# A binarised 3x3 convolution after group norm: a pair's two half convolutions side by side on TensorE, one more input slot, thresholds on GpSimd

## What is computed

```python
def _gn(v, G=32, eps=1e-05):          # G == C: one group is one channel of one image
    ...
    return ((g - m) / jnp.sqrt(s + eps)).reshape(v.shape)

def _L0_conv_ref(X, W, beta, v, bias, stride):
    B = jnp.sign(W[None] - mean + us[:, None, None, None, None] * std)   # 5 sign filters
    alpha = jnp.linalg.solve(Bf.T @ Bf, Bf.T @ wf)
    W_eff = jnp.einsum('m,mhwio->hwio', alpha, B)
    ...
    for n in range(3):
        An = jnp.sign(jnp.clip(X + v[n], 0.0, 1.0) - 0.5)
        out = out + beta[n] * (conv(An) + sum_alpha * bias[n])
    return out

x = x + _L0_conv_ref(_gn(x), ...)
```

## Time and profile before

| | before |
|---|---|
| median of 3 runs | 194.65 us (194.5 to 195.14) |
| the profiled execution | 194.47 us, of it the span of the profile 192.7 us |
| busy: TensorE, VectorE, ScalarE, GpSimd | 90%, 85%, 80%, 29% of the span |
| DMA over the span | 39.6 MB, mean 206 GB/s |

### The profile page before, as it was taken

How to read it: one execution, slowest core, us unless ns; L and a number is a source line. 1 busy time by engine, 2 the same in 40 slices (tenths; PEclk the granted TensorE clock), 3 DMA queues, 4 the chain that set the end, 5 groups by cost and what they waited for, 6 DMA issues and landing times.

```text
span 192.7 us, 4809 instructions
## 1 busy us (share of the span) xinstructions
PE 174.0 (90%) x1828; PEld 133.8 (69%) x1828; DVE 163.3 (85%) x409; ACT 154.2 (80%) x221; POOL 55.1 (29%) x72
## 2 busy tenths in 40 slices
PE   1898988749999999999899989999989999999992
PEld 1687765634868787868677777878777857677671
DVE  5579995999999999999988999899999899975242
ACT  2719968998898989999998989998988898872131
POOL 6264010006060606060605051323232242434000
PEclk9999999997999999999999999999999999999999
DMA  5999990063598989799988798989883837677725
GB/s 160 246 236 241 250 229 18 2 173 99 146 226 248 237 282 243 231 227 301 254 263 235 227 252 252 231 253 250 259 242 112 236 100 201 177 211 210 224 76 167
DMA packets 20476, 39.60 MB, mean 206 GB/s; under 512 B 9078, under 2 KB 9302, under 8 KB 20454
## 3 DMA queue, kind: packets, MB, share of 16 engines
q1 hardware_dynamic: 20144, 39.27, 74.8%
q10 hardware_dynamic: 310, 0.04, 0.1%
HBM read 13.15 MB, written 12.85 MB: 135 GB/s over the span
## 4 chain that ended last, share of the span: by engine, by line
PE 59%; DVE 18%; DMA 11%; ACT 7%; issue 2%; SPq 2%; DVEq 0%
PE conv_ps L843 33%; PE y_ps L876 10%; DMA s_odd<-s_even 10%; PE x_ps L795 6%; DVE raw_stats L629 5%; ACT signs L372 3%; DVE y_nat L620 3%; PE conv_ps L851 3%; DVE s_even L682 3%; PE conv_ps L846 2%; ACT x_ch L367 1%; ACT w_parts L413 1%; SPq L225 1%; ACT filt L410 1%; PE conv_ps L931 1%
## 5 line engine op out<-in xcount | busy, mean ns | idle before, releaser
L843 PE MATMUL conv_ps<-s_even,w_mm 128*64 128x448 f16 (+1 forms) x576 | 104.3, 335 | 3.5 <-DMA s_odd<-s_even 2.5
L846 PE MATMUL conv_ps<-s_odd,w_mm 128*64 128x448 f16 (+2 forms) x576 | 104.4, 323 | 0.0
L372 ACT ACTIVATE signs<-x_ch,neg_thr 128x784 f16<-128x784 f32 x96 | 85.3, 939 | 0.5
L843 PEld LDWEIGHTS conv_ps<-s_even,w_mm 128*64 128x64 f16 x576 | 60.6, 110 | 31.8 <-issue 10.3
L846 PEld LDWEIGHTS conv_ps<-s_odd,w_mm 128*64 128x64 f16 x576 | 60.8, 111 | 0.1
L335 POOL TENSOR_SCALAR lo_part<-signs,ratio_lo 128x1568 f16<-128x1568 f16 x14 | 22.0, 1575 | 103.1 <-DVE half_hi L675 103.1
L385 ACT ACTIVATE y_ch<-conv_ps,y_scale 128x896 f32<-128x896 f32 (+1 forms) x31 | 28.3, 911 | 17.6 <-PE conv_ps L851 10.3
L620 DVE SCALAR_TENSOR_TENSOR y_nat<-y_ps,y_const,x_nat 112x1024 f32<-112x1024 f32 (+1 forms) x30 | 34.4, 1148 | 8.3 <-PE y_ps L876 8.0
L629 DVE BATCH_NORM_STATS2 raw_stats<-x_ch 128x6 f32<-128x448 f32 (+1 forms) x64 | 31.6, 554 | 0.8 <-ACT x_ch L367 0.8
L876 PE MATMUL y_ps<-ident,y_ch 128*112 128x128 f32 x210 | 29.0, 278 | 0.0
L795 PE MATMUL x_ps<-ident,x_nat 112*128 112x112 f32 x192 | 25.5, 277 | 2.1 <-DMA x_nat<-in_x 1.4
(11 more groups left out here) (126 smaller groups left out, 126.7 us busy)
## 6 DMA issues: line engine op xcount, KB each, us to landing
x_nat<-in_x SPq DMA_DIRECT2D x16, 448.0 KB, 5.9
out<-y_nat SPq DMA_DIRECT2D x16, 448.0 KB, 5.9
s_odd<-s_even SPq DMA_DIRECT2D x32, 203.0 KB, 3.4
s_odd<-s_even SPq DMA_DIRECT2D x32, 188.5 KB, 3.8
x_nat<-in_x SPq DMA_DIRECT2D x16, 336.0 KB, 4.8
out<-y_nat SPq DMA_DIRECT2D x15, 322.0 KB, 2.9
s_odd<-s_even SPq DMA_DIRECT2D x16, 29.0 KB, 3.3
x_nat<-in_x SPq DMA_DIRECT2D x16, 14.0 KB, 5.9
```

What stands on the lines that cost most here:

```text
L372: act.activation(signs[q % 2][:, n, :, a, :], x_ch[q % CH_SLOTS][:, :, a, :], ACT.Sign, bias=neg_thr[q % 2][:, n, a:a + 1]).then_inc(signe ...
L843: last = nc.tensor.matmul(low[:, 0:n * ROWS], wt, s_even[b][:, part, r0:r0 + 2 * n, t:t + H], start=first, stop=end)
L846: last = nc.tensor.matmul(high[:, 0:m * ROWS], wt, s_odd[b][:, part, r0:r0 + 2 * m, t:t + H], start=first, stop=end and not at_edge)
```

## The change

The loop is written anew on all engines. A step on TensorE is now: half A of pair p, half B of pair p, statistics of pair p + 3, half B of pair p - 1 out, half B of pair p + 4 in (through `conv_ps[0]`, which half A has left), half A of pair p + 5 in, half A of pair p out. So all float16 matmuls of a pair stand together and all float32 work stands together, and half B leaves one period later; `y_ch` of half B has two buffers for that. The zero columns of `s_even` and `s_odd` are gone (rows of 56): the outer taps read and write 55 of 56 positions, and which tap starts and ends a bank is chosen so that it covers all of them. The two additions on VectorE write whole rows. The thresholds are computed on GpSimd (`thresholds`: one addition, one product, one sum and two `tensor_scalar`, L333 to L341) from the root and its inverse; VectorE keeps only the inverse. GpSimd's low part of a pair waits for `signed` and for `weigh_second` in place of `sum_half`. `x_nat` has 8 slots in place of 7, and the loop ahead of the steps loads all of them.

```diff
-X_SLOTS, CH_SLOTS, S_SLOTS = 7, 4, 3
+X_SLOTS, CH_SLOTS, S_SLOTS = 8, 4, 3
...
             for q in range(1, X_SLOTS):
                 load_x(q, 0)
                 load_x(q, 1)
...
+            def thresholds(q):
+                pool.wait_ge(moments_ready, 2 * (q + 1))
+                ts(var_eps[:], moments[q % 2][:, :, 1], GN_EPS, 1.0, ALU.add, ALU.mult).then_inc(pool_dev, 1)
+                pool.wait_ge(inverse_root, q + 1)
+                pool.wait_ge(pool_dev, 3 * q + 1)
+                tt(ratio_root[:], var_eps[:], inv_root[:], ALU.mult).then_inc(pool_dev, 1)
+                pool.wait_ge(pool_dev, 3 * q + 2)
+                tt(twice_dev[:], ratio_root[:], root[:], ALU.add).then_inc(pool_dev, 1)
+                pool.wait_ge(pool_dev, 3 * q + 3)
+                for a in range(2):
+                    ts(neg_thr[q % 2][:, :, a], order[:, 1, :], twice_dev[:, a:a + 1], moments[q % 2][:, a, 0:1],
+                       ALU.mult, ALU.add).then_inc(thr_ready, 1)
...
             for q in range(2, PAIRS):
-                weigh_low(q)
+                weigh_low_first(q)
+                weigh_low_second(q)
+                if q + 1 < PAIRS:
+                    thresholds(q + 1)
...
+            TAP_ORDER = [(1, 0, 2), (1, 0, 2), (0, 2, 1)]
+            TAP_OUT = [slice(1, H), slice(0, H), slice(0, H - 1)]
+            TAP_IN = [slice(0, H - 1), slice(0, H), slice(1, H)]
...
             def bring_out(p, f, ps=y_ps):
                 k = 2 * p + f
                 pe.wait_ge(y_scaled, k + 1)
                 if k:
                     pe.wait_ge(y_added, k)
-                if f == 0 and real(p - 1) and real(p + 3):
+                if f == 0 and real(p + 3):
                     pe.wait_ge(moments_ready, 2 * (p + 4))
...
             def step(p):
-                r, t = p + 3, p + 4
+                convolve(p, 0)
+                if p == 0:
+                    gather_lanes(2)
+                    pe.wait_ge(moments_ready, 6)
+                    bring_in(4, 0, x_ps, 7)
...
+                convolve(p, 1)
+                if p and real(p + 3):
+                    gather_lanes(p + 3)
+                if real(p - 1):
+                    bring_out(p - 1, 1)
+                if real(p + 4):
+                    pe.wait_ge(y_scaled, 2 * p + 1)
+                    bring_in(p + 4, 1, conv_ps[0], 0)
+                if real(p + 5):
+                    bring_in(p + 5, 0, x_ps, 2 * (p + 4) + 1)
+                if p == 0:
+                    gather_lanes(3)
+                bring_out(p, 0)
```

The steps of VectorE, ScalarE and SP follow the same period:

```diff
             def step(p):                     # VectorE
+                if real(p - 1):
+                    add_x(p - 1, 0)
+                if real(p + 1):
+                    sum_high(p + 1)
+                    sum_low(p + 1)
+                if real(p + 3):
+                    lane_moments(p + 3, 0)
+                    lane_moments(p + 3, 1)
+                    spread_lanes(p + 3)
+                if real(p + 2):
+                    weigh_first(p + 2)
+                    weigh_second(p + 2)
+                if real(p - 1):
+                    add_x(p - 1, 1)
+                if real(p + 3):
+                    pair_moments(p + 3)
+                if real(p + 2):
+                    sum_half(p + 2)
+                if real(p + 3):
+                    invert_root(p + 3)
...
             def step(p):                     # ScalarE
+                if real(p + 1):
+                    sign(p + 1, 0)
...
+                if real(p + 4):
+                    copy_in(p + 4, 0)
+                if real(p + 2):
+                    begin_signs(p + 2)
...
+                scale_out(p, 0)
+                if real(p + 2):
+                    sign(p + 2, 2)
...
+                    scale_out(p, 1)
+                if real(p + 4):
+                    copy_in(p + 4, 1, conv_ps[0])
+                if real(p + 3):
+                    take_root(p + 3)
```

More of the change, by code:

```diff
@@ L465, in _ @@
             copy_in(3, 0)
-            for p in range(-1, PAIRS):
+            take_root(2)
+            for p in range(PAIRS):
                 step(p)
@@ L778, in _ @@
             output_const()
-            for p in range(-1, PAIRS):
+            weigh_first(1)
+            pair_moments(2)
+            weigh_second(1)
+            sum_half(1)
+            invert_root(2)
+            weigh_low(1, 1)
+            weigh_low(1, 2)
+            for p in range(PAIRS):
                 step(p)
+            add_x(LAST, 0, x_ps)
+            add_last(0)
+            add_last(1)
         @block.tensor
@@ L957, in _ @@
             warm_up()
-            for p in range(-1, PAIRS):
+            bring_in(3, 1, y_ps, 6)
+            for p in range(PAIRS):
                 step(p)
```

231 lines of the change are left out of this document (80 added, 151 removed).

## The result

The changed kernel takes **218.4 us** (median of 4 runs, 217.94 to 222.01) against 194.89 for the kernel before beside it: a ratio of 1.120, 95% interval 1.114 to 1.126. It is slower, as forecast, but by 23.5 us where the forecast said 2.5. The time lies far outside the range of 194.2 to 200.8.

A forecast was written before the change was run, and what follows sets the result against it. Bound: a two-pair loop of TensorE, VectorE and the copy to s_odd. Copies -3.3, eighth slot +3.3, clock +0.7, rest of first periods -0.2, last periods +2.1, end -0.1: +2.5, median 197.1 us, range 194.2 to 200.8.

The forecast's parts named there:

- The thresholds: GpSimd in the loop: five small instructions run beside the rest on an otherwise unused engine, at a cost of nothing.
- (d): Rival, VectorE in the loop: half sum loses 0.5 us per period to GpSimd's product, total 200.4; chance 0.10.
- TensorE's own period: TensorE in the loop: fewer type switches (-0.18) and no zero columns (-0.07) bring the period from 9.67 to 9.42 us.
- the wait ahead of A's output: TensorE in the loop: moments of pair p + 3 need 2.14 us against 2.18 of work, a tie, 0.05 added.
- The copies: Copies to s_odd behind queued loads: 9.65 us for eight periods, 9.47 for two; -3.3 us, ends -4.8 and -0.3.
- The eighth slot: Start of pair 0: one more load queued ahead of its second copy delays half A; +3.3 us, ends 0 and 3.5.
- The clock: First periods: the half-clock dip in A of pair 1 recurs, a new one may come; +0.7 us, between 0 and 1.3.
- pair 0 to pair 2: First two periods: clock +0.7 us, and -0.2 for the rest, with four small VectorE instructions less.
- Rival (c): TensorE in the loop: float32 work in one piece brings a 1.3 us clock dip every third period, 203 us; chance 0.10.
- The last periods: End of the loop: B's output, its addition and A's output follow each other on one buffer, uncovered; +2.1 us.
- what is behind the last half A: End of the kernel, after the last half A: the order stays; -0.1 us.

The follow-up runs named there:

- thr_back: Changed kernel with the thresholds made on VectorE and ScalarE again, as before the change; 197.91 us, ratio 1.011 to the kernel before.
- thr_ahead: Changed kernel with GpSimd's thresholds ahead of both low products and VectorE's statistics ahead of its two sums; 202.49 us.
- tb_pads: thr_back with the zero columns kept (rows of 58, every tap on all 56 positions); 200.44 us, ratio 1.017.
- slots7: Changed kernel with seven input slots in place of eight; 217.18 us, ratio 1.113 to the kernel before.
- tb_tail7: thr_back with seven input slots and, in the last periods, half B's output in x_ps; 194.92 us, ratio 0.997.
- twice3: Changed kernel with GpSimd's small sum for the thresholds made three times in a row in every pair; 227.25 us, ratio 1.165.
- b_thr_pool: Kernel before the change with only the thresholds moved to GpSimd, behind both low products; 239.22 us, ratio 1.228.
- thr_stats: Changed kernel with thresholds between GpSimd's two low products and statistics ahead of VectorE's two sums; 204.67 us, ratio 1.035.
- stats_first: Changed kernel with only VectorE's order altered, statistics ahead of the two sums; 206.71 us, ratio 1.058.

## Why the prediction was wrong, step by step

**The thresholds (taken at nothing, measured 20.5 us).** This is the step that failed: "The thresholds' own five small instructions run beside these on GpSimd, which nothing else uses then." It asked whether GpSimd was free, not what stands ahead of them in its queue. Ahead stands the second product, which waits for the second weight, which waits for signs made from the thresholds of one pair earlier. That is a loop over one pair. The trace of before held all its pieces but the small ones, and it was never added up. The thresholds moved back give 20.5 us back (thr_back), and in the undisturbed periods another place in the queue does so too (thr_ahead). The rival on GpSimd's side (d) had the right pair of engines and the wrong victim: the half sum does lose 0.5 us (1.45 for 0.92), but the loop is set by the small instructions that VectorE holds. The earlier trace rows showed the hold on VectorE, 1.1 us; I never turned it round. The Trainium skill ("SBUF — State Buffer", "Who interferes with whom") says that whoever issues first has the shared pair for the whole instruction and that a `tensor_scalar` in a two-port mode takes it as well. The held weights of 1.63 and 1.73 us agree; the earlier trace rows alone didn't show that case. That the first to issue has the pair isn't seen in the threshold instruction, which by the recorded starts was 0.40 us ahead of the sum that held it.

**TensorE's own period (forecast 9.42 and a wait of 0.05, measured 9.60).** The work came out as forecast, and the wait ahead of A's output is what was mis-sized. In thr_ahead (TensorE's weight loads, then VectorE):

```profile
108.84 0.81 PEld L803 LDWEIGHTS x_ps<-ident,x_nat 112*128 112x128 f32 x8
109.89 0.84 PEld L891 LDWEIGHTS y_ps<-ident,y_ch 128*112 128x112 f32 x8 [0.24 <-issue]
```

```profile
109.50 0.28 DVE L670 BATCH_NORM_AGGREGATE moments<-y_ps 128x2 f32<-128x12 f32 x2
```

The moments are done at 109.78 and the output starts 0.11 us later, with 0.24 us of nothing to load before it; it is the same, within 0.01 us, in every period with both inputs in thr_ahead and thr_back. From the start of B's output to that of A's it takes 2.24 us (107.68 to 109.92), where the forecast had 2.14. TensorE's own work in it is 0.68 + 0.58 + 0.77 = 2.03, where the forecast had 2.18. The near tie is a wait of 0.2 us, and without it the period would be 9.4. Of what was won, the columns are 0.09 (tb_pads). That this wait makes the 9.60 is read from the traces; no run takes it away.

**The copies (forecast 9.65 for eight periods).** In thr_back, where this step can be seen, ten periods took 97.80 against the 96.1 of the forecast: the term is -1.7, within its ends. But its reason was wrong. TensorE waited for a copy once in ten periods, for 0.6 us, while VectorE was busy for 94.72 of 97.80. In seven of the ten, TensorE's weight loads wait for VectorE's statistics:

```profile
PEld y_ps L816 <- DVE spread_stats L647: 2.0, 7, 0.4
```

The upper end of -0.3 was not worked out: eight periods of 9.87 us, the forecast's own worst, and two of 9.47 give -1.6. That the measured size lies beside this is luck.

**The eighth slot (forecast +3.3, ends 0 and 3.5; the slot alone +1.2, the start of pair 0 here +1.9).** Right as a queue, mis-sized by the rate, as shown above; the rest of the 1.9 us goes with the half clock ahead of pair 0. One execution, that of thr_ahead, shows the forecast's own picture, with 4.97 us of idle up to 34.15.

**The clock (forecast +0.7).** The expected half clock in half A of pair 1 came, from 44.2 to 51.0 in place of 42.6 to 46.0, and a new one ahead of pair 0, from 23.7 to 30.6, behind an idle of 2.01 us. The same idle of 2.01 us passed without one in slots7 and thr_ahead. It stands behind 16 warm-up matmuls that took 2.05 us here and 3.78 before, with a granted clock of 1.00 recorded for both; why they differ is open. From pair 0 to pair 2 thr_back takes 25.65 us, 0.67 more than before. In the changed kernel it is 3.1 more; 2.4 of them are gone in thr_back, but there the second stretch at half clock is shorter too (44.1 to 47.5), and the two aren't separated. Rival (c), a dip in every third period, didn't come: 1.00 from 59 to 170 us, with all float32 work in one piece.

**The last periods (forecast 9.45, 9.13, 9.13; +2.1).** In thr_back 9.71, 9.18, 9.19: +2.5. Right in mechanism, as tb_tail7 shows. In the changed kernel GpSimd's loop goes on there, 11.29 and 11.36 us for two of the three, and the granted clock falls to half twice, from 170.5 to 173.9 and from 191.0 to 194.4, behind idle stretches of 2.33 and 2.51 us; from the start of half A of pair 12 to the statistics behind half B it took 7.81 us where the loop had 6.12.

By its own steps the forecast describes thr_back, the change without its thresholds: 197.1 forecast, 197.9 measured. That these are so close is in part luck. In the profiled execution of thr_back the start of pair 0 came 1.6 us later (forecast 3.3) and ten periods gave 1.7 (forecast 3.3), two misses that cancel; pair 0 to pair 2 cost 0.7 (0.5), the last periods 2.5 (2.1), what is behind the last half A 0.6 (-0.1). That the forecast named the right direction says nothing for it either: 20.5 of the 23.5 us come from a term that it put at nothing.

## What to carry to other kernels

A small instruction moved to another engine is priced by what stands ahead of it in that engine's queue and by who waits for its result; follow both until they meet, and if they meet within one period, add up the loop. An engine that is idle 70% of the time can still close a loop. Where two engines hold each other, take the hold in both directions, at its full length, and for the smallest instruction too; if several such instructions of the other engine follow each other, it can last over all of them.

## What the runs showed of the hardware

- A GpSimd instruction of 0.33 us took 2.47 us across two VectorE additions of 0.96 us that followed each other, in the changed kernel, and one of 0.20 us took 2.33 in twice3. In b_thr_pool one of 0.20 us took 0.92 and was let go between the two additions.
- The hold isn't limited to VectorE instructions with two inputs from SBUF: a float16 `tensor_scalar` of 0.63 us took 1.63 (thr_stats) to 1.73 (stats_first) beside a GpSimd product. Beside statistics, two threshold instructions of GpSimd took their own 0.67.
- Full DMA queues moved 233 to 279 GB/s from 2 to 24 us in executions with the same loads, and a copy behind them landed after 10.1 to 4.7 us.
- TensorE's granted clock fell to half behind idle stretches of 2.0 to 4.0 us at the start of the changed kernel, though not behind one of 2.0 in slots7. In its loop, in which TensorE idles for some 1.6 us in each period, it stayed at 1.00 for over 100 us. In twice3 it fell to half behind idle stretches of 1.99 us that began at 69.85, 93.27, 128.29 and 152.11, and not behind one of 1.99 us from 116.62.
